# Conditioning projections as three one-pass float32r products of split operands, in a fused attention and feed-forward kernel

## The reference

```
query = seq2 + b_self
key = concat([seq1 + b_prev, seq2 + b_self], 1)
value = concat([seq1, seq2], 1)
q = query @ Wq + bq
k = key @ Wk + bk
v = value @ Wv + bv
...
x = x + ffn_ref(cond_ref(x, side, lens, ...), ...)
```

## Time and profile before

| | |
|---|---|
| median of 3 runs | 3531.86 us (3531.86 to 3533.28) |
| profiled execution, first to last instruction | 3530.7 us |
| mean granted TensorE clock of it | 0.988 |
| PE busy | 3456.5 us, 98% |
| DVE busy | 2573.7 us, 73% |
| ACT busy | 2312.5 us, 65% |
| POOL busy | 742.2 us, 21% |
| length of one steady pass (240.0 to 3116.2 us, 27 passes) | 106.5 us |

### The profile page before, as it was taken

How to read it: one execution, slowest core, us unless ns; L and a number is a source line. 1 busy time by engine, 2 the same in 40 slices (tenths; PEclk the granted TensorE clock), 3 DMA queues, 4 the chain that set the end, 5 groups by cost and what they waited for, 6 DMA issues and landing times.

```text
span 3530.7 us, 58337 instructions
## 1 busy us (share of the span) xinstructions
PE 3456.5 (98%) x20452; PEld 2423.6 (69%) x20452; DVE 2573.7 (73%) x7101; ACT 2312.5 (65%) x5077; POOL 742.2 (21%) x882
## 2 busy tenths in 40 slices
PE   7899999999999999999999999999999999999997
PEld 4566776767776667777667777667767667767665
DVE  4577777777777777777777777777777777777764
ACT  2466766766766766766766766766666766666764
POOL 2221222121222122222112222112222212222111
PEclk8899999999999999999999999999999999999999
DMA  5210111111111101111101111101111101111000
GB/s 170 34 24 15 19 31 31 31 25 17 21 31 31 31 21 18 25 31 31 31 21 18 25 31 31 31 21 18 25 31 31 31 17 18 29 31 25 7 7 10
DMA packets 99201, 99.56 MB, mean 28 GB/s; under 512 B 9568, under 2 KB 97504, under 8 KB 98912
## 3 DMA queue, kind: packets, MB, share of 16 engines
q1 hardware_dynamic: 97552, 93.36, 15.2%
q10 hardware_dynamic: 1360, 2.47, 0.2%
HBM read 36.02 MB, written 8.39 MB: 13 GB/s over the span
## 4 chain that ended last, share of the span: by engine, by line
PE 88%; DVE 6%; ACT 4%; issue 2%; DMA 0%; POOL 0%; SPq 0%; POOLq 0%; ACTq 0%; DVEq 0%
PE ps L1114 14%; PE ps L1009 12%; PE ps L1125 8%; PE ps L1090 6%; PE ps L1023 6%; PE ps L1080 5%; PE ps L1069 5%; PE ps L1058 4%; PE ps L924 4%; PE ps L914 3%; PE ps L897 3%; PE ps L1043 3%; PE ps L868 3%; ACT attn_area L746 3%; PE ps L860 2%; PE ps L949 2%
## 5 line engine op out<-in xcount | busy, mean ns | idle before, releaser
L625 POOL TENSOR_TENSOR inv<-ssq_f,minus_half 128x16 f32<-128x16 f32 x128 | 419.4, 3276 | 1057.2 <-DVE ssq_f L1320 1057.1
L746 ACT ACTIVATE attn_area<-attn_area,f_nb,inv 128x128 f32<-128x128 f32 (+1 forms) x1024 | 546.1, 536 | 117.4 <-DVE f_nb L1348 116.6
L1114 PE MATMUL ps<-feed_area,w_s 128*128 128x256 f32 x2560 | 606.1, 382 | 4.2 <-DVE feed_area L1383 3.7
L1114 PEld LDWEIGHTS ps<-feed_area,w_s 128*128 128x128 f32 x2560 | 467.4, 190 | 88.0 <-issue 25.4
L1257 DVE TENSOR_REDUCE c_mx<-ps 128x2 f32<-128x512 f32 x512 | 348.7, 687 | 134.5 <-PE ps L897 132.5
L699 ACT ACTIVATE cond_area<-ps 128x512 f32<-128x512 f32 x512 | 298.9, 592 | 62.4 <-PE ps L914 59.1
L1344 DVE CUSTOM_DVE_ANT_0 attn_area<-ps,cst 128x128 f32<-128x128 f32 (+1 forms) x1024 | 303.4, 351 | 43.3 <-issue 41.2
L1394 DVE SCALAR_TENSOR_TENSOR feed_area<-ps,b_s,feed_area 128x256 f32<-128x256 f32 (+1 forms) x448 | 213.7, 477 | 138.8 <-ACT feed_area L772 123.0
L1125 PE MATMUL ps<-feed_area,w_s 128*128 128x256 f32 x1280 | 293.9, 381 | 0.3 <-DVE feed_area L1394 0.3
L1359 DVE TENSOR_SCALAR attn_area<-attn_area,f_inv 128x128 f32<-128x128 f32 (+1 forms) x1024 | 258.0, 315 | 9.1
L470 DVE COPY attn_area<-ps 128x384 f32<-128x384 f32 x256 | 141.8, 554 | 165.5 <-PE ps L1069 165.4
(11 more groups left out here) (144 smaller groups left out, 6516.0 us busy)
## 6 DMA issues: line engine op xcount, KB each, us to landing
cond_area<-cond_area SPq DMA_DIRECT2D x384, 128.0 KB, 4.6
res_rows<-in_x SPq DMA_DIRECT2D x32, 256.0 KB, 2.7
out<-res_rows SPq DMA_DIRECT2D x32, 256.0 KB, 2.1
x_rows<-in_x SPq DMA_DIRECT2D x31, 256.0 KB, 2.7
f_rows<-in_side SPq DMA_DIRECT2D x31, 256.0 KB, 3.0
wqkv_s<-in_wqkv SPq DMA_DIRECT2D x2, 1536.0 KB, 9.7
cond_area<-cond_area SPq DMA_DIRECT2D x128, 6.0 KB
w_s<-in_w SPq DMA_DIRECT2D x2, 768.0 KB, 12.3
```

The source lines that it names most:

```text
L625: nc.gpsimd.tensor_tensor(inv[:, l, t, :], ssq_f[:, l, t, :], minus_half[:, :], ALU.pow).then_inc(SL[l]["inv_norm"], 1)
L746: nc.scalar.activation(soft[:, h % SOFT, lo:hi], soft[:, h % SOFT, lo:hi], ACT.Exp, bias=f_nb[:, l, q, h:h + 1], scale=inv[:, l, q, h:h + ...
L1114: last = mm(ps[:, N0 + f % 2, c * N:(c + 1) * N], w1_s[:, l, k, lo:lo + P], hn[:, k, :], start=(k == 0), stop=(k == KD - 1))
```

## The change

The weights are loaded into `cw_raw`. DVE rounds them to float32r (`cw_high`, a cast) and subtracts that from the weights (`cw_low`, in the place of `cw_raw`), for each of the three matrices once, in pass 0. The transposed inputs are split in the same way for each sequence: the DVE copy and the ACT copy now write float32r (`in_T`, named `in_high`), and DVE subtracts both from the PSUM banks into `in_low`. Each float32 product becomes three float32r products: high by low, low by high, and high by high, into the same PSUM tile. PE's `project` 0 now waits for both subtractions (`in_split`). The two bias products of the setup stay float32 and are made twice, of the low and of the high weights. The conditioning area and the split inputs get fixed addresses. The order strings are the same.

```diff
@@ PER
-    in_turned=2, in_copied_dve=1, in_copied_act=1,
+    in_turned=2, in_high_dve=1, in_high_act=1, in_split=2,
@@ tiles
-        cw_s = sb("cw_s", [P, KD, 3 * D])
+        cw_raw, cw_low = (nc.alloc_sbuf_tensor_at(name, [P, KD, 3 * D], dt, offset=COND_AT - 4 * KD * 3 * D)
+                          for name, dt in (("cw_raw", F32), ("cw_low", F32R)))
+        cw_high = sb("cw_high", [P, KD, 3 * D], F32R)
@@ tensor engine
+            def products(to, held, moved):
+                for k in range(KD):
+                    for a, b in ((1, 0), (0, 1), (0, 0)):
+                        last = mm(to, held(k, a), moved(k, b), start=(k == 0 and a == 1),
+                                  stop=(k == KD - 1 and a + b == 0))
+                return last
...
             def key_biases():
                 pe.wait_ge(cols_loaded, 16)
                 pe.wait_ge(wk_loaded, 16)
+                pe.wait_ge(cw_split, 2)
...
                 elif name == "project":
                     if n == 0:
-                        pe.wait_ge(S["in_copied_dve"], upto(seq, "in_copied_dve", 1))
-                        pe.wait_ge(S["in_copied_act"], upto(seq, "in_copied_act", 1))
+                        pe.wait_ge(S["in_split"], upto(seq, "in_split", 2))
                         for b in range(KD):
-                            for k in range(KD):
-                                last = mm(ps[:, C0, b * N:(b + 1) * N], cw_s[:, k, D + b * P:D + (b + 1) * P],
-                                          in_T[:, 0, k, :], start=(k == 0), stop=(k == KD - 1))
+                            last = products(ps[:, C0, b * N:(b + 1) * N],
+                                            lambda k, a: (cw_high, cw_low)[a][:, k, D + b * P:D + (b + 1) * P],
+                                            lambda k, a: (in_T, in_low)[a][:, 0, k, :])
@@ vector engine
+            def split_weights(n, lo):
+                V.tensor_copy(cw_high[:, :, lo:lo + D], cw_raw[:, :, lo:lo + D]).then_inc(cw_split, 1)
+                dve.wait_ge(cw_split, 2 * n + 1)
+                V.tensor_tensor(cw_low[:, :, lo:lo + D], cw_raw[:, :, lo:lo + D], cw_high[:, :, lo:lo + D].bitcast(F32),
+                                ALU.subtract).then_inc(cw_split, 1)
...
                 if name == "rows":
                     dve.wait_ge(S["in_turned"], upto(seq, "in_turned", 1))
                     V.tensor_copy(in_T[:, 0], ps[:, C0, :].rearrange("p (k t) -> p k t", k=KD)
-                                  ).then_inc(S["in_copied_dve"], 1)
+                                  ).then_inc(S["in_high_dve"], 1)
+                    for s, high in enumerate(("in_high_dve", "in_high_act")):
+                        dve.wait_ge(S[high], upto(seq, high, 1))
+                        V.tensor_tensor(in_low[:, s], ps[:, C0 + s, :].rearrange("p (k t) -> p k t", k=KD),
+                                        in_T[:, s].bitcast(F32), ALU.subtract).then_inc(S["in_split"], 1)
```

More of the change, by code:

```diff
@@ L9 @@
 BF16 = mybir.dt.bfloat16
+F32R = mybir.dt.float32r
 I32 = mybir.dt.int32
@@ L23 @@
 VW = 32
+COND_AT = 229344 - 4 * 11776
 C_SCALE = 1.0 / np.sqrt(CDH)
@@ L314, in adaln_ffn_kernel, with __init__ @@
         class Area:
[L315 to L316 removed]
+            def __init__(self, name, cols, offset=None):
+                self.ap = sb(name, [P, cols]) if offset is None else nc.alloc_sbuf_tensor_at(name, [P, cols], F32, offset=offset)
+                self.at, self.cols = 0, cols
             def take(self, cols):
@@ L321, in take @@
                 return self.ap[:, self.at - cols:self.at]
-        front = Area("cond_area", 11776)
+        front = Area("cond_area", 11776, COND_AT)
         attn = Area("attn_area", 11264)
         feed = Area("feed_area", 4096)
-        in_T = front.take(2 * KD * N).rearrange("p (s k t) -> p s k t", s=2, k=KD)
+        in_T, in_low = (nc.alloc_sbuf_tensor_at(name, [P, 2, KD, N], F32R, offset=COND_AT + 4 * front.at
+                                                + 4 * 2 * KD * N * a) for a, name in enumerate(("in_high", "in_low")))
+        front.take(2 * 2 * KD * N)
         qk_c = front.take(TILES * 2 * D).rearrange("p (t c) -> p t c", t=TILES)
@@ L651, in _ @@
                 act.dma_start(rows[:, :, :], src[0:1].rearrange("b (t p) d -> p (b t) d", p=P)).then_inc(S[loaded], 16)
-            load(cw_s[:, :, 2 * D:3 * D], wv, wv_loaded)
+            load(cw_raw[:, :, 2 * D:3 * D], wv, wv_loaded)
             load(cwo_s[:, :, :], cwo, wv_loaded)
@@ L678, in cond @@
                     nc.scalar.activation(in_T[:, 1], ps[:, C0 + 1, :].rearrange("p (k t) -> p k t", k=KD),
-                                         ACT.Copy).then_inc(S["in_copied_act"], 1)
+                                         ACT.Copy).then_inc(S["in_high_act"], 1)
                 elif name == "part" and n == 1:
@@ L793, in key_biases @@
                 pe.wait_ge(wk_loaded, 16)
+                pe.wait_ge(cw_split, 2)
                 for b in range(KD):
                     for k in range(KD):
-                        last = mm(ps[:, R0, b:b + 1], cw_s[:, k, D + b * P:D + (b + 1) * P],
-                                  cols[:, V_PREV + k:V_PREV + k + 1], start=(k == 0), stop=(k == KD - 1))
+                        for w in (cw_low, cw_high):
+                            last = mm(ps[:, R0, b:b + 1], w[:, k, D + b * P:D + (b + 1) * P].bitcast(F32),
+                                      cols[:, V_PREV + k:V_PREV + k + 1], start=(k == 0 and w is cw_low),
+                                      stop=(k == KD - 1 and w is cw_high))
                 last.then_inc(bias_product, 1)
@@ L802, in row_biases @@
                 pe.wait_ge(wq_loaded, 16)
+                pe.wait_ge(cw_split, 4)
                 for k in range(KD):
-                    last = mm(ps[:, T0, :], bwide[:, k, :], cw_s[:, k, 0:2 * D], start=(k == 0), stop=(k == KD - 1))
+                    for w in (cw_low, cw_high):
+                        last = mm(ps[:, T0, :], bwide[:, k, :], w[:, k, 0:2 * D].bitcast(F32), start=(k == 0 and w is cw_low),
+                                  stop=(k == KD - 1 and w is cw_high))
                 last.then_inc(bias_product, 1)
@@ L808, in wv_there @@
                 pe.wait_ge(wv_loaded, 48)
+                pe.wait_ge(cw_split, 6)
             def b1_products(l):
@@ L866, in cond @@
                             pe.wait_ge(S["key_rest"], upto(seq, "key_rest", KD))
-                        for k in range(KD):
-                            last = mm(ps[:, C0 + n % 2, :], in_T[:, 1, k, t * P:(t + 1) * P],
-                                      cw_s[:, k, 0:2 * D], start=(k == 0), stop=(k == KD - 1))
+                        last = products(ps[:, C0 + n % 2, :],
+                                        lambda k, a: (in_T, in_low)[a][:, 1, k, t * P:(t + 1) * P],
+                                        lambda k, a: (cw_high, cw_low)[a][:, k, 0:2 * D])
                     else:
@@ L876, in cond @@
                         for t in range(TILES):
-                            for k in range(KD):
-                                last = mm(ps[:, C0 + s, t * D:(t + 1) * D], in_T[:, s, k, t * P:(t + 1) * P],
-                                          cw_s[:, k, 2 * D:3 * D], start=(k == 0), stop=(k == KD - 1))
+                            last = products(ps[:, C0 + s, t * D:(t + 1) * D],
+                                            lambda k, a: (in_T, in_low)[a][:, s, k, t * P:(t + 1) * P],
+                                            lambda k, a: (cw_high, cw_low)[a][:, k, 2 * D:3 * D])
                     last.then_inc(S["projected"], 1)
@@ L1147, in _, with key_weights @@
             V = nc.vector
+            def split_weights(n, lo):
[3 more added lines that the diff above has]
+                                ALU.subtract).then_inc(cw_split, 1)
+            def key_weights():
+                dve.wait_ge(wk_loaded, 16)
+                split_weights(0, D)
             def key_side():
@@ L1159, in masks @@
             def masks():
+                dve.wait_ge(wq_loaded, 16)
+                split_weights(1, 0)
                 V.tensor_copy(ident_h[:, :], ident)
@@ L1408, in step @@
                 (cond if name in CONDITIONING else layer)(seq, name, n)
-            run(dve, "DVE", step, {(0, "part", 1): key_side, (0, "project", 1): masks, (0, "project", 3): values_there,
+            run(dve, "DVE", step, {(0, "rows", 0): key_weights, (0, "part", 1): key_side, (0, "project", 1): masks, (0, "project", 3): values_there,
                                    (0, "score", 0): rotation_tables, (0, "rotate", (0, 0)): turns_made,
```

6 lines of the change are left out of this document (4 added, 2 removed).

## The result

| | before | changed |
|---|---|---|
| median | 3531.94 us (3531.86 to 3533.28) | 3563.02 us (3559.45 to 3563.77) |
| span of the profiled execution | 3530.7 us | 3561.6 us |
| PE busy | 3456.5 us | 3433.8 us |
| DVE busy | 2573.7 us | 2609.4 us |
| first turn of a steady pass | 240.0 us | 253.4 us |

The ratio is 1.0083, 95% interval [1.0068, 1.0097]: 0.83% slower. The forecast was 3554.7, the range 3536 to 3578. PE works 22.7 us less in the whole run and ends 31 us later.

The account below looks back on a forecast made before the run. PE was taken to set the time, with a chain DVE, ACT, DVE beside it only 0.42 us from making it wait. 3530.7 + 16.8 (steady passes) + 6 (setup) = 3553.5, median 1.2 above: 3554.7 us, range 3536 to 3578.

Parts of the forecast that it names:

- The sign and its mechanism: Steady pass: subtractions delay the chain DVE, ACT, DVE, PE waits, each pass grows by 0.58 us; slower given 0.85.
- The credit of the first `f_nb`: DVE behind `soften`: the moved `f_nb` avoids POOL's line 638, takes 0.16 instead of 0.53, and 0.36 us come back.
- The products: PE's `project` 0 to 4: float32r at 0.11 us for 256 columns, 0.22 for 512, PE's work 2.0 us a pass less.
- rival 3: `project` 3 and 4: weight loads set 0.19 us per 256-column product, lag 1.16 a pass, 3572 us with setup; 7%.
- the setup: First pass: key weights' split, doubled bias products and query weights' split, less cheaper projections, 5.8 us, taken as 6.
- upper bound: Setup: at most 10 us, if the weights' cast is held beside POOL's memset as a two-port instruction was for 3.6.
- the value split: First pass: the value weights' split, with passes 1 and 2, set at nothing, with 2 us either way.
- rival 1: Steady pass: PE decides after all, the 2.0 us a pass stay saved, 3480 us; 7%.
- rival 2: DVE's subtractions take half of line 1221's time, the chain is later by nothing, 3532 us with a hidden setup; 4%.
- rival 4: PE's projections: no one-pass mode, two passes for each product, 4.32 us a pass, about 3667 us; 5%.
- the steady part: 29 steady passes, each longer by 0.58 us: 16.8 us.
- the step from the profiled span to the median: The median lies 1.2 us above the span of the profiled execution.

Follow-up runs that it names:

- Experiments 1 to 3: Changed kernel with one float32 product of high halves for each three (3560.64 us); without both input subtractions (3532.93 us); with only the subtraction of `x` (3543.66 us).
- Experiment 5: Experiment 4 with DVE's `soften` of layer 1 moved ahead of `rows`: 3547.26 us, ratio 1.0040 to the kernel before.
- experiment 6: Experiment 5 with POOL's product of queries and own keys issued at `project` 2, ahead of the inverse norms: 3514.69 us, ratio 0.9948.
- Experiment 4: Changed kernel with the query and value weight splits moved ahead of the waits for bias products on DVE: 3554.06 us, ratio 1.0060.
- experiments 4 to 7 and 9: Runs with early weight splits; the last is experiment 6 plus PE's variance product ahead of `project` 0 and DVE's normalization ahead of its turned-probabilities copy: 3501.5 us.
- experiments 7 and 10: Experiment 6 with PE's line 1031 block ahead of the turn: 3554.95 us; float32 kernel before with `soften`, own-key, variance and normalization moves: 3530.9 us.

## Why the prediction was right, and where it was off

**The sign and its mechanism.** PE was busy for less and the run was longer, because a chain DVE, ACT, DVE beside PE had less room than the subtractions take. The forecast had `soften` 1.32 us late (1.32), the exponentials 0.96 (0.96), line 1383 0.62 (0.63), line 1114 0.58 (0.60), the turn behind `project` 4 0.58 (0.66). The credit of the first `f_nb`, short because POOL is through by then, was there: 0.17 in place of 0.53. Experiments 1 to 3 show the cause and not only the pattern: without subtractions a pass is shorter than before the change (106.21), with one it is as before (106.54), and with float32 products it is as long as in the changed kernel. Experiment 5 moved them behind `soften` and took back 0.30 a pass; experiment 6 took 1.07 by POOL's place alone. So the last wait hung on an `f_nb` that POOL held for 1.08. The prediction had seen that chain only as one that moves along with PE's turns; the held `f_nb` in it was in the trace before, and it had not looked there.

**The products.** 0.118 and 0.2325 us, where 0.11 and 0.22 stood. The blocks save 0.09 (`project` 0, which starts 0.1 late behind `in_low` and whose first product takes 0.23), 0.32, 0.33 and 0.61 (3 and 4, where 24 products take 2.83 us in place of 3.44): 1.35 us a pass in place of 2.0. It didn't matter for the time, since it is all waited away; it shows in the waits, in full 0.72 for ACT where 1.0 was forecast and 0.51 ahead of the hidden product where 0.7 was. The two blocks that now start behind a wait (lines 1031 and 1136) take 0.10 and 0.05 longer than before. So 1.86 more of waiting and these 0.15, less 1.35 saved, give 0.66, beside 0.65 measured. The bound of 0.19 from the weight loads (rival 3) is refuted by this row, though its records are as long as those of float32:

```profile
L801 PEld LDWEIGHTS ps<-cw_low,in_high 128*128 128x128 f32 x384 | 73.7, 192 | 5.7 <-issue 1.4
```

**The step that failed is the setup:** 6 taken, 13.4 measured, beyond even the 10 given as its upper bound. The first scores in the kernel before:

```profile
30.54 1.03 PE L897 MATMUL ps<-cond_area 97*128 97x256 bf16 x4 [2.77 <-DMA cond_area<-cond_area]
```

Until there PE is 13.3 us later (43.85). In parts, from the starts on PE: 0.6 to the first bias product, 1.8 for the key bias products (1.6 forecast), 4.6 of waiting for the query weights, 3.5 for the row bias products (2.6 forecast), 4.0 of waiting for the value weights, 1.65 for the value products, less 2.9 in other places (0.8 in `project` 0, 0.3 in `project` 1 and 2, 1.8 ahead of the scores, where the wait of 2.77 for DMA is gone). The prediction added durations of DVE and PE as if the splits followed the work; it did not ask where in DVE's list the two later splits stand. They stand behind steps that themselves wait for PE and ACT, and PE waits for them in turn. It set the value split at nothing without naming its cover. The upper bound came from one held instruction, not from two waits and the halved clock behind each. Experiment 4 took back 8.7 of it by moving the splits.

These are single profiled executions, and the first passes scatter. With the splits at the same place the first steady turn came at 253.43, 255.56, 253.67 and 250.56 us (changed kernel, experiments 1 to 3), with the early splits at 244.74, 246.81, 243.68, 241.99 and 244.97 (experiments 4 to 7 and 9). The two groups do not meet, and even the least growth over 240.0 is above 10, but 13.4 and 8.7 are good to some 3 us only.

**The rivals.** PE did not decide (rival 1), the splits were not hidden (rival 2), and a product is one pass (rival 4). Weight loads did not decide either (rival 3, above). The result lies 8.3 us above the forecast: 7.4 are the setup, 0.7 the steady part, and 0.2 the step from the profiled span to the median, taken as 1.2 and measured as 1.4.

## What to carry to other kernels

Before making the busiest engine's work cheaper, list how long the chains beside it are and where the added work stands in their lists; 1.35 us of saved matmul was worth nothing until the order was made for it. Work that follows another step in an in-order list starts when that step has waited, so a setup's splits go where their data arrive and not where they are wanted. Read each move twice, once for what the moved instruction waits for and once for who waits for it, as experiments 7 and 10 show.

## What the runs showed of the hardware

- A float32r product takes 0.118 us for 256 columns and 0.2325 for 512, at a granted clock of 1.00, with weight loads whose records last 192 ns but whose successors start 0.118 apart. The Trainium skill (FP8 and Floating Point Precision, section TensorE Precision Notes) has true float32 as four passes and names a reduced form without a rate; a float32 product of 256 columns takes 0.43 us here, 3.6 times as long, near the page's four.
- The cast of the key weights took 1.22 us and ended 0.28 behind POOL's memset of 3.51; the same cast took 0.42 where it had started ahead of POOL's product (15.79 against 15.95). So a memset held it too. It did not hold the subtraction with two SBUF inputs: that took 0.69 us at 6.33, beside POOL's next memset (6.07 to 9.74).
- Nor does every POOL instruction that reads SBUF hold one with two SBUF inputs. DVE's sum of line 1369 took 1.22 us at 271.67, inside POOL's power instruction (line 633, 3.29 us from 270.50), and its product of the same size, line 1352, took 1.21 at 267.87 with POOL idle. Here the trace differs from the rule cited in experiment 6.
- The clock that PE is granted fell to 0.51 and 0.50 behind waits of 4.4 and 3.8 us, as the rows of the first pass show. In experiment 4, without these waits, it was 1.00 from 15.4, where its record starts, to 28.0 us.
- The clock's record starts late: at 13.4 us in the kernel before, 13.6 in the changed one, 15.4 in experiment 4 and 23.3 in experiment 1. The profile prints 1.00 for what lies ahead of it, but PE takes twice its steady time there. The products of 10.57 to 13.3 us stand 0.21 apart, not 0.118, and `project` 0 of the kernel before takes 3.6 us (8.1 to 11.68) against 1.72 in a steady pass. In experiment 1 a row bias product of 512 columns takes 1.71 us at 20.59 and 0.86 at 23.65, on either side of the first record:

```profile
20.59 1.91 PE L823 MATMUL ps<-cw_high,attn_area 128*128 128x512 f32 x2
...
23.65 1.02 PE L823 MATMUL ps<-cw_high,attn_area 128*128 128x512 f32 x2
```

By these durations PE stands at its lower level, 1.2 GHz, until the first record.
